# A gap of 320 bytes in on-chip memory before the second of two split input tiles

## The reference, cut to what matters

```
x = x + tanh(g_xattn) * xattn(layernorm(x), ctx)
x = x + tanh(g_ffn)   * ffn(layernorm(x))

xattn:  q = rope(rms(x Wq)), 16 heads of 128;  k = rope(rms([ctx, x] Wk)), v = [ctx, x] Wv, 4 heads of 128
        softmax(q k / sqrt(128)) v, then Wo
ffn:    softmax router over 8 experts, the best 2 of width 176, plus a shared expert of width 352
...
```

## Time and profile before

| what | value |
|---|---|
| time, median of 3 runs | 1236.16 us (1235.7 to 1237.02) |
| span of the profiled execution | 1234.9 us |
| TensorE matmul, busy | 1210.5 us (98%), 8781 instructions |
| TensorE weight load, busy | 1141.9 us (92%) |
| VectorE, busy | 1008.0 us (82%) |
| GpSimd, busy | 919.6 us (74%) |
| ScalarE, busy | 885.3 us (72%) |

### The profile page before, as it was taken

One profiled execution on the slowest core, in us unless ns is written; L12 is line 12 of the kernel. 1 busy time (PEld: TensorE's weight loads), 2 busy tenths in 40 slices (PEclk: granted clock), 3 DMA queues, 4 the chain that ended last, 5 costly groups with the idle time before them and its releaser, 6 DMA issues.

```text
span 1234.9 us, 31490 instructions
## 1 busy us (share of the span) xinstructions
PE 1210.5 (98%) x8781; PEld 1141.9 (92%) x8782; DVE 1008.0 (82%) x2992; ACT 885.3 (72%) x3754; POOL 919.6 (74%) x1124
## 2 busy tenths in 40 slices
PE   6899999999999999999999999999999999999998
PEld 3788999999999999999999999999999999999997
DVE  8788888888888888888888888888888677777443
ACT  7978777777777777777777777777777546666322
POOL 2678887888888888888888887888887425555654
PEclk9999999999999999999999999999999999999999
DMA  6634233322222322222333333322236536554574
GB/s 179 196 105 131 78 105 105 106 89 89 89 89 89 94 89 89 94 89 93 109 109 102 101 100 119 101 75 75 75 109 205 199 103 187 162 162 146 186 239 151
DMA packets 128792, 148.57 MB, mean 120 GB/s; under 512 B 13824, under 2 KB 108288, under 8 KB 127968
## 3 DMA queue, kind: packets, MB, share of 16 engines
q1 hardware_dynamic: 122256, 130.16, 34.8%
q0 software_dynamic: 6480, 17.77, 3.9%
HBM read 66.93 MB, written 80.76 MB: 120 GB/s over the span
## 4 chain that ended last, share of the span: by engine, by line
PE 95%; ACT 2%; DVE 2%; issue 1%; another core or an unknown queue 0%; DMA 0%; SPq 0%; DVEq 0%; ACTq 0%
PE b_kv L1711 14%; PE b_q L1697 14%; PE b_o L1795 13%; PE b_sc L1769 9%; PE b_aT L1784 9%; PE b_pT L1777 5%; PE b_qT L1758 4%; PE b_q L2031 3%; PE b_kv L2031 3%; PE b_q L1828 2%; PE b_kT L1754 2%; PE b_kT L1828 2%; PE b_aT L1946 1%; PE b_pT L2048 1%; PE b_aT L2048 1%; PE b_o L1747 1%
## 5 line engine op out<-in xcount | busy, mean ns | idle before, releaser
L1711 PE MATMUL b_kv<-w_group,kv_in_hi 128*128 128x256 f32 x992 | 205.5, 305 | 0.0
L747 POOL TENSOR_TENSOR qk_r<-qk_me,minus_half 128x6 f32<-128x6 f32 x128 | 173.7, 1357 | 10.1 <-POOL qk_me L745 0.2
L957 ACT ACTIVATE probs<-b_sc,neg_max 128x128 f32<-128x128 f32 x512 | 180.5, 373 | 0.1
L751 POOL TENSOR_TENSOR q_rot<-q_rot,q_sin 128x512 f32<-128x512 f32 x128 | 163.8, 1279 | 6.8 <-DVE q_sin L1273 1.9
L1711 PEld LDWEIGHTS b_kv<-w_group,kv_in_hi 128*128 128x128 f32 x992 | 161.8, 190 | 6.7 <-issue 0.4
L1697 PE MATMUL b_q<-w_group,kv_in_hi 128*128 128x512 f32 x496 | 164.9, 413 | 0.0
L951 ACT ACTIVATE pT<-b_pT 128x512 f32<-128x512 f32 x128 | 76.7, 599 | 102.9 <-PE b_pT L1777 100.9
L1795 PE MATMUL b_o<-wo_hi,aT_hi 128*128 128x256 f32 x480 | 143.5, 299 | 0.1
L1769 PE MATMUL b_sc<-kT,qT 128*128 128x128 f32 x1024 | 135.8, 275 | 6.2 <-ACT qT L946 4.2
L754 POOL TENSOR_TENSOR q_rot<-q_rot,qk_r 128x512 f32<-128x512 f32 x128 | 133.5, 1043 | 10.0
L1711 PE MATMUL b_kv<-w_group,kv_in_lo 128*128 128x256 f32 x496 | 139.6, 281 | 0.0
(11 more groups left out here) (309 smaller groups left out, 3949.2 us busy)
## 6 DMA issues: line engine op xcount, KB each, us to landing
xs_scratch<-zeros SPq DMA_DIRECT2D x34, 1032.0 KB, 6.2
s_in<-xs_scratch SPq DMA_DIRECT2D x71, 129.0 KB
yT_scratch<-yT SPq DMA_DIRECT2D x32, 256.0 KB
yS<-yT_scratch SPq DMA_DIRECT2D x32, 256.0 KB
routed<-ys_scratch SPq DMA_DIRECT2D x32, 256.0 KB, 3.6
w_hi_all<-w_scratch SPq DMA_DIRECT2D x3, 1536.0 KB, 14.0
x_in<-in_x SPq DMA_DIRECT2D x32, 128.0 KB, 2.3
ctx_raw<-in_ctxT SPq DMA_DIRECT2D x32, 128.0 KB, 2.6
```

The costliest lines, as they stand in the source:

```text
L747: nc.gpsimd.tensor_tensor(qk_r[g % 2][:], qk_me[:], minus_half[:, 0:REP + NB], ALU.pow).then_inc(r_ready, 1)
L751: nc.gpsimd.tensor_tensor(q_rot[g % 2][:], q_rot[g % 2][:], q_sin[g % 2][:], ALU.add) \
L957: last = nc.scalar.activation(probs[:, j, :], b_sc[:, j * P:(j + 1) * P], ACT.Exp, bias=neg_max[g % 2][:, j:j + 1], accum_out=row_sum[g % ...
L1711: last = nc.tensor.matmul(b_kv[:, s * 2 * HD:(s + 1) * 2 * HD], kv_in[p][a][:, c, 2 * s:2 * s + 2, :], wkv_of(b, c)[:, g % KVH, :], start= ...
```

## The change

One tile of 80 floats (320 bytes) that nothing reads or writes is allocated between `kv_in0` and `kv_in1`. No instruction is added, removed or moved. `kv_in1` and every tile that the cursor places after it, and the tiles of the second phase that start from `free_at` or `late_at`, move up by 320 bytes. `ring_at` was taken ahead of the gap, so `yS4` to `yS7` stay. So does everything ahead of `kv_in1`: `w_group`, `wo`, the raw and low weights, `ident`, `x_n`, `hT`.

```
         ring_at = list(cursor)
-        kv_in = [parts(f"kv_in{p}", [P, DC, 4, S]) for p in range(2)]
+        kv_in = [parts("kv_in0", [P, DC, 4, S])]
+        kv_gap = sb("kv_gap", [P, 80], F32)
+        kv_in.append(parts("kv_in1", [P, DC, 4, S]))
         ring_end = cursor[0]
```

## The result

The changed kernel takes 1249.3 us, median of 4 runs (1248.64 to 1249.8), against 1236.59 us before (median of 4 runs, one more than in the table ahead): a ratio of 1.0106 with a 95% interval of 1.0094 to 1.0118, so 12.7 us slower. The forecast was 1230.0 us, in a range of 1226.5 to 1241. The sign was wrong, and the time lies outside the range. Two lines were added ahead of the functions, so what was line 1711 before is line 1713 now, 1697 is 1699, 1795 is 1797 and 1291 is 1293.

What follows compares the result with a forecast made beforehand. The prediction took TensorE's matmul starts to bound the kernel: −4.2 us (`keys_values`) and −2.0 us (slots' down product) on a 1234.9 us span gave 1228.7, plus 1.3 to the median of runs, 1230.0 us; range 1226.5 to 1241.

Steps and rivals of the forecast that it cites:

- What bounds the kernel, and that an address changes a distance: Whole kernel: time is the sum of distances between TensorE matmul starts, and operand addresses change these by about 5.5 ns.
- nothing depends on the address: Rival for all matmuls: addresses are worth 0 us, giving 1236.2 us; chance 0.24.
- Point 1: `keys_values` of odd tiles, 768 matmuls: `kv_in1`'s new residue saves 5.5 ns each, 4.2 us less (bounds 0 and 4.6).
- Point 2: `queries` of odd tiles, 384 matmuls of 512 columns: taken as 0, bounds 2.3 us gain or a loss the same size.
- Point 3: `project`, 1440 matmuls, as `aT` moves from 128 to 448: taken as 0, other end 7.9 us more.
- Point 4: Slots' down product, 355 matmuls of 256 columns, as `s_hT` moves from 64 to 384: 2.0 us less, or 0.
- Sum: All parts of the change added: −4.2 − 2.0 = −6.2 us on the 1234.9 us span.
- Point 7: Other engines' and DMAs' accesses at moved addresses: taken as covered by VectorE's 7 us spare in 60, more on others.
- the second (keys and values fast, projection slow): Rival: `kv_in1` and `s_hT` become fast, `aT` slow, +1.7 us, 1237.9 us; chance 0.20.
- The third: Rival: `project` loses its good place and `keys_values` gains none, price 7.9 us, 1244.1 us; chance 0.12.

Runs made afterwards that it cites:

- m1: TensorE alone, no part of the reference: 16 weight-load/matmul pairs per group, stationary at 8 residues, moving at 3, widths 256, 352, 512; 256 columns gave 113.3 to 120.0 ns.
- f2: Kernel before, without GpSimd's cosine tables from the third tile on: 1234.1 us, 1.0000 of before.
- f1: Changed kernel, without GpSimd's cosine tables from the third tile on: 1237.9 us, 1.0032 of before.
- e2: Kernel before with the 320 bytes placed behind `kv_in1`, which stays, so only later tiles move: 1248.4 us, 1.0112 of before.
- e7: Kernel before, addresses unmoved, plus one idle 16-column matmul behind the projection in groups 0 and 2: 1250.3 against 1236.4 us, 1.0110.
- e5: Changed kernel with GpSimd's cosine table moved behind its two short layer-norm operations: 1253.5 us, 1.0134 of before.
- e6: Kernel before with GpSimd's cosine table moved behind its two short layer-norm operations: 1254.5 us, 1.0141 of before.
- m2: TensorE alone, 256 columns, four address differences, each after no lead-in or 4 matmuls of 16, 128 or 512 columns: 113.3 or 117.8 ns at the same addresses.

## Why the prediction was wrong

- **What bounds the kernel, and that an address changes a distance: right.** m1 shows it with nothing but TensorE running. The rival "nothing depends on the address" is refuted. The section of the Trainium skill that it leaned on (SBUF — State Buffer, "Who interferes with whom") calls TensorE's two read ports independent; for this kind of matmul the runs don't agree, since the distance goes by the difference of the two addresses (m1, 113.3 to 120.0 ns at 256 columns). Its other sentence, that TensorE never waits on anyone, is about other engines, and m1 has none beside it.
- **Point 1, `keys_values` of odd tiles: right sign, mis-sized.** 2.3 ns × 768 = 1.8 us where 4.2 were forecast. The step between the two kinds of place is 5.0 ns as a mean over all groups (118.9 less 113.9), not 5.5, and D = 192 has a second rhythm of 117.8 ns, in which three groups of four are.
- **Point 2, `queries`: taken as 0, it was 2.5 ns × 384 = 1.0 us more,** inside its bound of 2.3. At 512 columns D = 192 is the worst class, at 256 it shares the best.
- **Point 3, the first step that failed: the projection's D = 128 was taken as 0.** It cost 4.43 ns (118.35 less 113.92) × 1440 = 6.4 us. The bound of 7.9 was there. The choice between the ends went by 352-column rows, and m1 shows why that was wrong: the classes rank differently at each width, and D = 128 is the best at 352 columns, and at 256 it costs 119.2 ns.
- **Point 4, the slots' down product: right in kind, mis-sized.** Its distances went from 118 and 119 ns to 114 (one of them to 116), but the first distance of each five grew from 202 to 206. From the first slot's down product to the last one's it is 0.6 us less (141.0 to 140.5 us; f2 to f1 139.0 to 138.3) where 2.0 were forecast, and the end doesn't see it: from the start of tile 31's `keys_values` to the end it takes 297.5 us before and 297.8 after the change, 295.8 in both f2 and f1.
- **Sum:** the products of points 1 to 3 give 6.4 − 1.8 + 1.0 = 5.6 us, too much, because they leave out the first distance of each group. With every distance inside the groups of f1 and f2 counted it is 5.1 for `project`, −2.2 for `keys_values` and 1.1 for `queries`, 4.0 us in all, against 3.8 us measured between the two runs.
- **Point 7, the second step that failed and the larger one: "VectorE has 7 us in 60 to spare".** That is an average over groups. In group 0 of an odd tile the slack behind the multiply was less than the 0.87 us by which it was held up, and whether it is held up hung on 27 to 48 ns of lead. A tile in which it is held up takes 29.96 us instead of f1's 29.31, so some 0.2 us of the 0.87 were slack and 0.65 reach the end. The stretch from the start of tile 4's `keys_values` to that of tile 31's holds 15 such tiles; it takes 789.3 us before, 793.4 in f1 and 803.0 in the changed kernel. So there the addresses cost 4.1 us and the collision 9.6; the rest of the two profiled executions differs by half a microsecond the other way. No term, bound or rival of the prediction had the collision, and so the range was too narrow.
- **What would have been luck:** without the collision the time would have been about 1240.5 us (an estimate: f1's 1.0032 of 1236.6), inside the range and with the wrong sign.
- **The rivals:** the second (keys and values fast, projection slow) named the right places, but as 1.7 us and 1237.9, with nothing of the collision. The third had the right sign and 1244.1 us, for a reason that isn't the one found.

How the slower matmuls turn the order can be read from the timelines of tile 19, as the time from the start of the tile's first `queries` to each of the two instructions (us):

| | multiply (VectorE) | table (GpSimd) |
|---|---|---|
| before | 17.21 | 17.25 |
| changed | 17.26 | 17.27 |
| e2 | 17.31 | 17.31 |
| e7 | 17.31 | 17.23 |

The multiply comes 0.06 to 0.11 us later with TensorE, the table at most 0.06 later; so a lead of 0.04 us is gone. Why GpSimd doesn't follow the whole delay was not taken apart: probably because the multiply follows the exponentials and these follow the scores, while GpSimd's list of work hangs on earlier work of TensorE. That is argued, not shown.

## What to carry to other kernels

Padding in front of a tile moves every tile behind it, so list the residues of all operands that move, and cost each at its own matmul width; a tile nobody meant to touch (`aT` here) can carry the result. Before trusting that a small delay is hidden, look in the timeline for pairs on VectorE and GpSimd that start within some 50 ns of each other and of which one is stretched (1.40 for 1.01 us): there some 40 ns decided who waits, and slack averaged over a stretch says nothing about the engine that may lose. Don't look for such a loss in the busy share or in the table of waits, which both stood still here, but in the chain and in the distance from tile to tile. When a change moves the time by more than its own instructions can, knock out the suspected partner in both kernels and compare the two; merely moving it (e5, e6) can make a new collision.

## What the runs showed of the hardware that was not expected

- The distance of fp32r pairs of weight load and matmul goes by the moving less the stationary address mod 256: 113.3 or 117.8 ns (D = 64 and 192), 119.2 (128), 118.9 to 120.0 (0) at 256 columns, 227 to 233.5 at 512, 158 to 161 at 352 (m1, granted clock 1.00, the upper level of 2.4 GHz).
- At D = 64 and 192 the same addresses have two steady rhythms, 113.3 and 117.8 ns, chosen by what ran before (m2); once settled they lasted to the end of the groups of 16.
- Two instructions of VectorE and GpSimd that started within 6 ns: the loser took 1.43 us instead of 0.56 (changed kernel). One of VectorE on 2 columns that started 0.23 us into GpSimd's table took 0.78 instead of 0.16 (e6).
